# The last of four batches in a one-core adaLN transformer block: second buffers, own PSUM banks, and each engine's order written out call by call

## The chip, the cores and the metric

One core of a Trainium2 chip runs the whole block as one launch. Time is device microseconds from the start to the end of one execution; less is better. The kernel before has a median of 464.82 us over three runs (464.00 to 464.89).

## What is computed

Four batches of 1024 tokens and 512 channels go through attention and a feed-forward step, both behind a layer norm that is scaled and shifted by a modulation vector of the batch, and both added back through a gate:

```python
mod = (silu(c) @ wmod).reshape(4, 6, 1, -1)          # sa, ca, ga, sb, cb, gb
ga, gb = [sign(g) * max(abs(g), 0.25) for g in (ga, gb)]
h = layernorm(x) * (1 + ca) + sa
qf, kf = h @ Wq.T, h @ Wk.T                          # 64 columns each
attn = softmax(16-times-the-same qf @ kf.T)          # one matrix for all 16 heads
x = x + ga * ((attn @ (h @ Wv.T)) @ Wo.T)
h = layernorm(x) * (1 + cb) + sb
x = x + gb * (h @ sum_r(factors[r]) / sqrt(8) + bias)
```

`head_f` is all ones, so every head has the same probabilities, and the kernel works with one probability matrix per batch and one product matrix of Wv and Wo.

## The kernel before

**Tiles.** The 4096 tokens are 32 tiles of 128 rows, eight per batch. Tiles 24 to 31 are the last batch. Every product is made in three matmuls of a `fp32r` upper part and a rest (`three`, L459 to L466: upper by rest, rest by upper, upper by upper), so each operand is kept twice, as `_hi` (rounded, written by ScalarE) and `_lo` (whole minus rounded, written by VectorE, helper line L1062).

**One tile's way.** For tile t: scores (4 matmuls of 512 columns into `ps_s`, two banks, L540 and L541), row maximum on VectorE (`row_max`, L1121), exponentials on ScalarE (`exponentials`, L804, into the single buffer `probs`), then a turn of the probabilities by 90 degrees. It goes through DRAM: one store from SyncE (`send_p`, L401), four loads (`fetch_p`, L409) into one half of `pb`, and a block transpose on VectorE (`turn_p`, L1196). Only tile 24 (and the first few) is turned on TensorE instead. ScalarE rounds the turned probabilities in two halves into `pt_hi` (`probs_part`), VectorE makes `pt_lo` (`probs_rest`), and `attend` runs 24 matmuls with the batch's values into `ps_o`. VectorE scales and gates the sum (`gate_attention`, L1156, into `attn`), adds it to the row in `x_ring` (`add_x`, L1164) and takes the layer norm's statistics (L1169, L1173). GpSimd makes the inverse deviation in three small instructions (`of_x1`, L1470 to L1474), ScalarE normalizes (`normalize_x1`, L830), another store and load through DRAM (L372, L377) and a block transpose (`turn_x1`, L1191) turn the tile, ScalarE modulates it (L756) into `h2_f` and rounds it (`h2_upper`), VectorE makes the rest (`h2_rest`), and `feed_forward` runs 12 matmuls into `ps_y`. ScalarE copies the sum out into the one buffer `ffn` (`ffn_out`, L865), and GpSimd adds the bias, multiplies by the gate and adds the row (`result`, L1487, L1493, L1497). SyncE stores tiles in pairs (`store_pair`, L313).

**What is single.** `ps_s`, `probs`, `ps_o`, `ps_y`, `attn`, `ffn`, `pt_hi`/`pt_lo`, `h2_hi`/`h2_lo` exist once; `v_hi` and `v_lo` hold 16 tiles, those of two batches, so the half of batch 2 is read by nobody once tile 23 has been attended.

**What sets the order.** Each engine runs its own written list and waits on semaphores that count what the others have done. The list is a step per tile. TensorE's step t in the last batch is:

```python
if turned_by_pe(t): transpose_probs(t)        # tile 24 alone
if t > T - TB: scores_of(scored_in(t))        # t + 2; none in step 30
feed_forward(t - 3)
if t == T - TB: scores_of(scored_in(t))
attend(t, g)
```

The other engines' steps of the last batch are `closing_step` on ScalarE and VectorE, `step` on SyncE and GpSimd. Behind step 31 stand the feed-forwards of tiles 29, 30 and 31, the last in two halves of 256 columns in `ps_y` and `ps_o` with VectorE making both parts in four pieces. `gated` (L1181) takes the scaling and the gate of tiles 29, 30 and 31 on VectorE, with the bias times the gate added ahead by GpSimd (`add_gated_bias`, L1515). Tiles 0 to 23 have other work besides: the values and keys of the next batch.

## Time and profile before

| | us |
|---|---|
| median of three runs | 464.82 |
| the profiled execution, its own time | 464.78 |
| its span in the trace | 463.0 |
| TensorE busy in the span | 450.1 |
| VectorE busy | 365.9 |
| ScalarE busy | 338.8 |
| GpSimd busy | 237.7 |

The granted TensorE clock is 1.00 throughout (the higher of its two levels, 2.4 GHz). The profiled execution lasted 1.8 us longer than its span. A matmul row's duration overlaps that of the next one: rows of 0.39 us start 0.23 us apart. So what a stretch of matmuls costs is read from the starts, and a stall is a start that comes later than that.

### The profile page before, as it was taken

Reading aid. Unit: us, or ns where it says so; the run is one execution under the profiler, and the core shown is the slowest. Engines: PE = TensorE matmul, PEld = TensorE weight load, DVE = VectorE, ACT = ScalarE, POOL = GpSimd, SP = SyncE. Lnnn points to the kernel's source line nnn. Section 1 sums busy time; section 2 is a strip of 40 time slices with the busy share of each in tenths; the row PEclk is TensorE's granted clock in tenths of the full one; section 3 lists DMA queues with packets and bytes.
Section 4 is the critical chain, followed back from the end, with each engine's and each line's share of the span. In section 5 each row is a group of like instructions: output and inputs, shape, how many; then the busy total and the mean of one; then the engine's idle time right before and its main releaser. Section 6 shows DMA issues by size and latency. Waiting matters only on the chain. (4 is left out here: it accounts for less than half of the span.)

```text
span 463.0 us, 7344 instructions
## 1 busy us (share of the span) xinstructions
PE 450.1 (97%) x2114; PEld 365.1 (79%) x2114; DVE 365.9 (79%) x641; ACT 338.8 (73%) x676; POOL 237.7 (51%) x307
## 2 busy tenths in 40 slices
PE   8989999999999999999999999999999999999996
PEld 5768778788888888888888888888888777777674
DVE  5988879678777878789787987798887577887765
ACT  5889777687868777778787786878786566567552
POOL 0347546152555554455565645454644475566662
PEclk9999999999999999999999999999999999999999
DMA  7999999634678365867677366877674237565512
GB/s 288 382 356 218 158 177 170 141 74 132 183 206 271 92 206 159 264 203 241 195 195 228 110 216 190 258 201 245 185 227 115 91 117 227 158 217 180 183 58 91
DMA packets 79160, 88.07 MB, mean 190 GB/s; under 512 B 4872, under 2 KB 55816, under 8 KB 79120
## 3 DMA queue, kind: packets, MB, share of 16 engines
q1 hardware_dynamic: 75168, 80.00, 56.5%
q0 software_dynamic: 3808, 7.34, 9.6%
q8 instruction: 17, 0.28, 0.2%
q10 hardware_dynamic: 144, 0.26, 0.2%
q14 instruction: 23, 0.19, 0.1%
HBM read 53.49 MB, written 34.10 MB: 189 GB/s over the span
## 5 line engine op out<-in xcount | busy, mean ns | idle before, releaser
L1470 POOL TENSOR_SCALAR ve<-mv 128x1 f32<-128x1 f32 x64 | 22.5, 351 | 165.7 <-DVE mv L1173 120.1
L464 PE MATMUL ps_o<-v_lo,pt_hi 128*128 128x512 f32 x256 | 100.2, 391 | 0.9 <-DVE pt_lo L1062 0.9
L466 PE MATMUL ps_o<-v_hi,pt_hi 128*128 128x512 f32 x256 | 99.7, 389 | 0.0
L465 PE MATMUL ps_o<-v_hi,pt_lo 128*128 128x512 f32 x256 | 99.6, 389 | 0.0
L1062 DVE TENSOR_TENSOR h_lo<-h_f,h_hi 128x512 fp32r<-128x512 f32 (+1 forms) x67 | 49.7, 741 | 12.2 <-ACT h_hi L728 11.6
L464 PEld LDWEIGHTS ps_o<-v_lo,pt_hi 128*128 128x128 f32 x256 | 48.0, 188 | 12.9 <-issue 2.9
L466 PEld LDWEIGHTS ps_o<-v_hi,pt_hi 128*128 128x128 f32 x256 | 48.0, 188 | 10.1
L465 PEld LDWEIGHTS ps_o<-v_hi,pt_lo 128*128 128x128 f32 x256 | 48.1, 188 | 9.7
L756 ACT ACTIVATE h_f<-x1b,mod_t 128x128 f32<-128x128 f32 x120 | 53.1, 596 | 2.8 <-DVE x1b L1191 2.5
L464 PE MATMUL ps_y<-f_lo,h_hi 128*128 128x512 f32 (+1 forms) x124 | 48.7, 393 | 2.3 <-issue 1.5
L465 PE MATMUL ps_y<-f_hi,h_lo 128*128 128x512 f32 (+1 forms) x124 | 47.9, 386 | 0.0
L466 PE MATMUL ps_y<-f_hi,h_hi 128*128 128x512 f32 (+1 forms) x124 | 47.9, 386 | 0.0
L1472 POOL TENSOR_TENSOR rstd<-ve,minus_half 128x1 f32<-128x1 f32 x64 | 44.8, 700 | 5.3
L756 ACT ACTIVATE h_f<-xb,mod_t 128x128 f32<-128x128 f32 x80 | 35.4, 593 | 12.9 <-DVE xb L1187 12.8
L464 PE MATMUL ps_v<-wvo_lo,h_hi 128*128 128x512 f32 x112 | 44.3, 396 | 0.0
L465 PE MATMUL ps_v<-wvo_hi,h_lo 128*128 128x512 f32 x112 | 43.8, 391 | 0.0
L1196 DVE STREAM_TRANSPOSE pb<-pb 128x1024 f32<-128x1024 f32 x24 | 29.8, 1241 | 17.6 <-DMA pb<-p_blocks 17.6
L466 PE MATMUL ps_v<-wvo_hi,h_hi 128*128 128x512 f32 x112 | 43.6, 390 | 0.0
L1487 POOL TENSOR_TENSOR ffn<-ffn,bias_bc 128x512 f32<-128x512 f32 x29 | 40.2, 1388 | 5.8 <-ACT ffn L865 5.8
L1497 POOL TENSOR_TENSOR x_ring<-ffn,x_ring 128x512 f32<-128x512 f32 x30 | 38.8, 1293 | 5.2 <-POOL ffn L1493 5.0
L1493 POOL TENSOR_TENSOR ffn<-ffn,gates 128x512 f32<-128x512 f32 x29 | 38.8, 1338 | 4.9 <-issue 4.5
L1121 DVE TENSOR_REDUCE negmax<-ps_s 128x1 f32<-128x1024 f32 x32 | 38.8, 1212 | 2.0 <-PE ps_s L541 1.8
(201 smaller groups left out, 1032.2 us busy)
## 6 DMA issues: line engine op xcount, KB each, us to landing
x_blocks<-xn SPq DMA_DIRECT2D x50, 256.0 KB, 2.7
p_blocks<-probs SPq DMA_DIRECT2D x24, 512.0 KB, 3.6
pb<-p_blocks SPq DMA_DIRECT2D x96, 128.0 KB, 3.2
x_ring<-in_x SPq DMA_DIRECT2D x16, 512.0 KB, 4.6
x1b<-x_blocks SPq DMA_DIRECT2D x30, 256.0 KB, 2.9
result<-x_ring SPq DMA_DIRECT2D x15, 512.0 KB, 3.0
f_sum<-in_factors POOLq DMA_DIRECT2D x14, 512.0 KB, 6.2
xb<-x_blocks SPq DMA_DIRECT2D x20, 256.0 KB, 2.9
```

The lines of the kernel that those rows point to most:

```text
L464: nc.tensor.matmul(acc, a_hi, b_lo, start=first, stop=False)
L465: nc.tensor.matmul(acc, a_lo, b_hi, start=False, stop=False)
L466: return nc.tensor.matmul(acc, a_hi, b_hi, start=False, stop=last)
L756: last = nc.scalar.activation(to[:, k, :].rearrange("p (c b) -> p b c", b=Q), turned[:, k], ACT.Identity, scale=mod_t[:, b, v + 1, k:k + 1 ...
L1062: return nc.vector.tensor_tensor(to, whole, full(hi), ALU.subtract)
L1121: nc.vector.tensor_reduce(negmax[:, t & 3:(t & 3) + 1], ps_s[:], AX_X, ALU.max, negate=True).then_inc(max_done, 1)
L1196: nc.vector.transpose(pb[:, n & 1, :], pb[:, n & 1, :]).then_inc(pb_turned, 1)
L1470: nc.gpsimd.tensor_scalar(ve[:, one], mv[:, u, 1:2], EPS, None, ALU.add).then_inc(ve_done, 1)
L1472: nc.gpsimd.tensor_tensor(rstd[:, one], ve[:, one], minus_half[:], ALU.pow).then_inc(rstd_done, 1)
L1487: nc.gpsimd.tensor_tensor(ffn[:], ffn[:], bias_bc[:], ALU.add).then_inc(biased_done, 1)
L1493: nc.gpsimd.tensor_tensor(ffn[:], ffn[:], gates[:, 1, b & 1, :], ALU.mult).then_inc(gated_done, 1)
L1497: nc.gpsimd.tensor_tensor(tile, ffn[:], tile, ALU.add).then_inc(y_done, 1)
```

## The change

Tiles 0 to 23 keep their order on all engines, but for the end of step 23, which is now part of the written-out list. For the last batch:

- `pt_hi`/`pt_lo` of odd tiles get a second home in `v_hi`/`v_lo`, slots 0 and 1; h2's parts rotate over three homes (slots 2 and 3, and the old one); `ffn` alternates with slot 0 of `x_ring`; `rden` has four columns.
- Attention of even tiles goes to `ps_qk`, of odd tiles to `ps_o`; feed-forward of odd tiles from 21 on to `ps_v`, of even ones to `ps_y`, of tile 30 to `ps_t[1]`, and the halves of tile 31 to the two banks of `ps_s`.
- Every engine's calls from the end of step 23 to the end of the kernel are written out one by one.

```diff
+        pt_homes = [(pt_hi[:], pt_lo[:]),
+                    tuple(v[:, 0:2, :].rearrange("p s (j i) -> p (s j) i", i=P) for v in (v_hi, v_lo))]
+        h2_homes = [tuple(v[:, i, :].rearrange("p (k i) -> p k i", i=P) for v in (v_hi, v_lo)) for i in (2, 3)]
+        h2_homes.append((h2_hi[:], h2_lo[:]))
+        ffn_homes = [ffn[:], x_ring[:, 0, :]]
-        last_banks = [ps_y, ps_o]
+        last_banks = [ps_s[:, 0:D // 2], ps_s[:, D:D + D // 2]]
...
+        late = TILES - PER_BATCH
+        def h2_of(t):
+            if t == T - 2:
+                return h2_next_to_last
+            return h2_homes[(t - late + 2) % 3 if t >= late - 2 else 2]
+        def ffn_of(t):
+            return ffn_homes[t % 2 if t >= late - 3 else 0]
+        def y_bank(t):
+            if t == T - 2:
+                return ps_t[1]
+            return ps_v if t >= late - 3 and t % 2 else ps_y
+        def o_bank(t):
+            return ps_qk if t >= late and t % 2 == 0 else ps_o
...
-                wait(pe, attn_done, t)
+                wait(pe, attn_done, t if t < late else t - 1)
...
-                    if j == 3 * TB // 4 and aside is not None:
+                    if j == HALF and aside is not None:
...
+            scores_of(25)
+            transpose_probs(24)
+            feed_forward(21)
+            scores_of(26)
+            attend(24, 12)
+            scores_of(27)
+            feed_forward(22)
+            attend(25, 12)
+            scores_of(28)
+            attend(26, 13)
+            scores_of(29)
+            feed_forward(23)
+            attend(27, 13)
+            scores_of(30)
+            feed_forward(24)
+            attend(28, 14, lambda: scores_of(31))
+            attend(29, 14)
+            feed_forward(25)
+            attend(30, 15, lambda: feed_forward(26))
+            attend(31, 15)
+            feed_forward(27)
+            transpose_last_but_one()
+            feed_forward(28)
+            feed_forward(29)
+            last_transpose()
+            feed_forward(30)
+            last_half(0)
+            last_half(1)
...
-                wait(act, y_acc, t)
+                wait(act, y_acc, t if t < late - 2 else t - 2)
...
-                wait(act, y_done, t)
-                nc.scalar.activation(ffn[:], ps_y[:], ACT.Identity, scale=FSCALE).then_inc(ffn_done, 1)
+                wait(act, y_done, t if t < late - 3 else t - 1)
+                if t == late - 3:
+                    act.wait_ge(y_stored, 16 * (PAIRS // 2 + 1))
+                nc.scalar.activation(ffn_of(t), y_bank(t)[:], ACT.Identity, scale=FSCALE).then_inc(ffn_done, 1)
...
+            def gate_third_last():
+                dve.wait_ge(y_acc, T - 2)
+                dve.wait_ge(y_done, T - 4)
+                gated(ffn_of(T - 3), y_bank(T - 3)[:]).then_inc(ffn_done, 1)
```

SyncE, from the exponentials of tile 25 on. `p_blocks<-probs` is a `send_p`, `pb<-p_blocks` a `fetch_p`, `x_blocks<-xn` a `send_x1`, `x1b<-x_blocks` a `fetch_x1`. Before:

```order
L401 DMA p_blocks<-probs 128x4x256
L409 DMA pb<-p_blocks 32x4x256 x4
L372 DMA x_blocks<-xn 128x4x128
L377 DMA x1b<-x_blocks 128x512
L401 DMA p_blocks<-probs 128x4x256
L409 DMA pb<-p_blocks 32x4x256 x4
L372 DMA x_blocks<-xn 128x4x128
```

Now:

```order
L429 DMA p_blocks<-probs 128x4x256
L437 DMA pb<-p_blocks 32x4x256 x4
L429 DMA p_blocks<-probs 128x4x256
L400 DMA x_blocks<-xn 128x4x128
L405 DMA x1b<-x_blocks 128x512
L437 DMA pb<-p_blocks 32x4x256 x4
L429 DMA p_blocks<-probs 128x4x256
L400 DMA x_blocks<-xn 128x4x128
L437 DMA pb<-p_blocks 32x4x256 x4
L405 DMA x1b<-x_blocks 128x512
```

The probabilities of tile 26 are now sent ahead of the trip of tile 23's rows, and those of tile 27 are fetched ahead of the rows of tile 24.

VectorE, from the gate of tile 23 on. Before:

```order
L1156 SCALAR_TENSOR_TENSOR attn<-ps_o,rden,gates 128x512
L1116 CAST qs_lo<-qk_lo 64x256
L1117 CAST qs_lo<-qk_lo 64x256
L1121 TENSOR_REDUCE negmax<-ps_s 128x1
L1164 TENSOR_TENSOR x_ring<-attn,x_ring 128x512
L1169 BN_STATS stats<-x_ring 128x6
L1173 BN_AGGR mv<-stats 128x2
L1062 TENSOR_TENSOR pt_lo<-ps_t,pt_hi 128x512 x2
L1191 STREAM_TRANSPOSE x1b<-x1b 128x512
L1149 RECIPROCAL rden<-rowsum 128x1
L1121 TENSOR_REDUCE negmax<-ps_s 128x1
L1196 STREAM_TRANSPOSE pb<-pb 128x1024
```

Now:

```order
L1307 SCALAR_TENSOR_TENSOR attn<-ps_o,rden,gates 128x512
L1268 TENSOR_REDUCE negmax<-ps_s 128x1
L1263 CAST qs_lo<-qk_lo 64x256
L1264 CAST qs_lo<-qk_lo 64x256
L1342 STREAM_TRANSPOSE x1b<-x1b 128x512
L1315 TENSOR_TENSOR x_ring<-attn,x_ring 128x512
L1209 TENSOR_TENSOR pt_lo<-ps_t,pt_hi 128x512
L1300 RECIPROCAL rden<-rowsum 128x1
L1320 BN_STATS stats<-x_ring 128x6
L1324 BN_AGGR mv<-stats 128x2
L1268 TENSOR_REDUCE negmax<-ps_s 128x1
L1209 TENSOR_TENSOR pt_lo<-ps_t,pt_hi 128x512
```

The row maximum of tile 25 comes first, and the two halves of `pt_lo` of tile 24 stand apart, one ahead of the statistics and one behind the maximum of tile 26.

VectorE, the last rows of the program. Before:

```order
L1181 SCALAR_TENSOR_TENSOR probs<-ps_v,gates 128x512
L1454 TENSOR_TENSOR x_ring<-probs,x_ring 128x512
L1181 SCALAR_TENSOR_TENSOR attn<-ps_y,gates 128x256
L1460 TENSOR_TENSOR x_ring<-attn,x1b 128x256
```

Now:

```order
L1332 SCALAR_TENSOR_TENSOR probs<-ps_t,gates 128x512
L1414 TENSOR_TENSOR x_ring<-probs,x_ring 128x512
L1332 SCALAR_TENSOR_TENSOR x_ring<-ps_v,gates 128x512
L1332 SCALAR_TENSOR_TENSOR attn<-ps_s,gates 128x256
L1425 TENSOR_TENSOR x_ring<-attn,x1b 128x256
```

The gate of tile 29 (`x_ring<-ps_v`, `gate_third_last`) stood ahead of the four pieces of tile 31 before, and now stands behind tile 30's and ahead of tile 31's halves.

## Rows read from the trace of the kernel before

**Rows 1.** The page, its first line.

```profile
span 463.0 us, 7344 instructions
```

**Rows 2.** Busy time by stretch: window, length, each engine's us (instructions), clock, DMA share, GB/s.

```profile
200.00:360.00 160.00, 159.96 (x748) 133.60 (x747) 134.49 (x228) 125.86 (x253) 85.11 (x113) 1.00 0.68 199
369.60:459.70 90.10, 84.62 (x370) 65.52 (x368) 67.75 (x110) 53.46 (x102) 54.56 (x58) 1.00 0.48 152
```

**Rows 3.** Timeline of TensorE, 358 to 369 us: start, us, what.

```profile
358.74 0.39 PE L464 MATMUL ps_y<-f_lo,h_hi 128*128 128x512 f32 x1
...
361.46 0.39 PE L540 MATMUL ps_s<-k_both,qs_lo 128*128 128x512 f32 x1
...
362.36 0.39 PE L464 MATMUL ps_o<-v_lo,pt_hi 128*128 128x512 f32 x1
...
367.80 0.39 PE L540 MATMUL ps_s<-k_both,qs_lo 128*128 128x512 f32 x1
...
368.71 1.03 PE L470 MATMUL ps_t<-ident,probs 128*128 128x128 f32 x8
```

**Rows 4.** Timeline of TensorE, 370 to 460 us: starts behind a stall, and the last.

```profile
370.58 0.47 PE L464 MATMUL ps_y<-f_lo,h_hi 128*128 128x512 f32 x1 [0.83 <-ACT ffn L865]
...
380.93 0.47 PE L540 MATMUL ps_s<-k_both,qs_lo 128*128 128x512 f32 x1 [0.90 <-ACT probs L804]
...
448.66 0.40 PE L466 MATMUL ps_o<-v_hi,pt_hi 128*128 128x512 f32 x1
...
454.61 0.66 PE L470 MATMUL ps_t<-ident,xn 128*128 128x128 f32 x4 [0.48 <-ACT xn L839]
...
459.44 0.28 PE L465 MATMUL ps_o<-f_hi,h_lo 128*128 128x256 f32 x1
459.56 0.28 PE L466 MATMUL ps_o<-f_hi,h_hi 128*128 128x256 f32 x1
```

**Rows 5.** Timeline of ScalarE, 371 to 376 us.

```profile
371.21 1.12 ACT L804 ACTIVATE probs<-ps_s,negmax 128x1024 f32<-128x1024 f32 x1 [0.78 <-DVE negmax L1121]
...
375.18 0.60 ACT L865 ACTIVATE ffn<-ps_y 128x512 f32<-128x512 f32 x1 [1.78 <-POOL x_ring L1497]
```

**Rows 6.** SyncE's and VectorE's timelines: the trip of tile 25's probabilities.

```profile
372.44 0.36 SPq L401 DMA_DIRECT2D p_blocks<-probs  x1
375.38 1.76 SPq L409 DMA_DIRECT2D pb<-p_blocks  x4
...
379.66 1.25 DVE L1196 STREAM_TRANSPOSE pb<-pb 128x1024 f32<-128x1024 f32 x1 [3.08 <-DMA pb<-p_blocks]
```

**Rows 7.** VectorE's groups, 369 to 460 us: xcount, busy us, mean ns.

```profile
L1062 DVE TENSOR_TENSOR h_lo<-h_f,h_hi 128x512 fp32r<-128x512 f32 x9 | 10.3, 1140 | 3.4 <-ACT h_hi L728 3.4
L1062 DVE TENSOR_TENSOR pt_lo<-pb,pt_hi 128x512 fp32r<-128x512 f32 x14 | 8.8, 671 | 0.0
L1121 DVE TENSOR_REDUCE negmax<-ps_s 128x1 f32<-128x1024 f32 x7 | 8.5, 1210 | 0.1
```

**Rows 8.** Timelines of GpSimd and VectorE at 371 us.

```profile
370.61 1.29 POOL L1487 TENSOR_TENSOR ffn<-ffn,bias_bc 128x512 f32<-128x512 f32 x1 [5.76 <-ACT ffn L865]
...
371.10 1.36 DVE L1164 TENSOR_TENSOR x_ring<-attn,x_ring 128x512 f32<-128x512 f32 x1
```

**Rows 9.** Timeline of all engines, 453 to 463 us.

```profile
453.67 1.27 POOL L1497 TENSOR_TENSOR x_ring<-ffn,x_ring 128x512 f32<-128x512 f32 x1
455.11 0.38 SPq L313 DMA_DIRECT2D result<-x_ring  x1
...
458.44 0.69 DVE L1454 TENSOR_TENSOR x_ring<-probs,x_ring 128x512 f32<-128x512 f32 x1
...
459.95 1.18 SPq L453 DMA_DIRECT2D result<-x_ring  x2
460.34 0.42 DVE L1460 TENSOR_TENSOR x_ring<-attn,x1b 128x256 f32<-128x256 f32 x1
```

**Rows 10.** DMA issues, 440 to 463 us: KB each, median us to landing.

```profile
result<-x_ring SPq DMA_DIRECT2D x1, 512.0 KB, 2.8
```

More of the change, by code:

```diff
@@ L561, in attend @@
                     v = [part[:, first + j, :] for part in (v_hi, v_lo)]
-                    last = three(ps_o[:], (pt_hi[:, j, :], pt_lo[:, j, :]), v, j == 0, j == TB - 1)
+                    last = three(o_bank(t)[:], [part[:, j, :] for part in pt_of(t)], v, j == 0, j == TB - 1)
                 last.then_inc(o_acc, 1)
@@ L583, in feed_forward, with last_half @@
                                  (f_hi[:, k, :], f_lo[:, k, :]), k == 0, k == C - 1)
+                last.then_inc(y_acc, 1)
+            def last_half(half):
+                pe.wait_ge(exp_done, T)
+                for k in range(C):
+                    if half == 0:
+                        pe.wait_ge(last_lo_done, k + 1)
+                    last = three(last_banks[half], [part[:, k, :] for part in h2_of(T - 1)],
+                                 [part[:, k, column_halves[half]] for part in (f_hi, f_lo)], k == 0, k == C - 1)
                 last.then_inc(y_acc, 1)
@@ L621, in step @@
                     ready()
[L622 to L623 removed]
+                attend(t, g)
+                if scored_last_in(t) is not None and t < T - TB - 1:
                     scores_of(scored_last_in(t))
@@ new lines, in _ @@
+            probs_part(26, 0)
+            probs_part(26, 1)
+            modulate_x1(23, batch_of(11))
+            h2_upper(23)
+            exponentials(28)
+            probs_part(27, 0)
+            ffn_out(22)
+            probs_part(27, 1)
+            normalize_x1(25, 1, False)
+            pair_q(15)
+            exponentials(29)
+            modulate_x1(24, batch_of(12))
+            h2_upper(24)
+            probs_part(28, 0)
+            probs_part(28, 1)
+            normalize_x1(26, 0, False)
@@ L1446, in _ @@
[L1446 to L1461 removed]
+            gate_attention(23, 1, 2)
@@ new lines, in _ @@
+            turn_x1(28)
+            gate_attention(30, 0, 3)
+            add_x(30)
+            x1_stats(30, 0)
+            h2_rest(28)
+            invert_sum(31, 1)
+            gate_attention(31, 1, 3)
+            turn_x1(29)
+            add_x(31)
+            x1_stats(31, 1)
+            add_last_bias()
+            h2_rest(29)
+            h2_rest(30, whole=h_f)
+            last_h2_parts(0)
+            last_h2_parts(1)
+            last_h2_parts(2)
+            last_h2_parts(3)
+            gate_next_to_last()
```

451 lines of the change are left out of this document (303 added, 148 removed).

## The prediction

> **What bounds the kernel now.** I first read busy time by stretch [rows 2]. Between 200 and 360 us TensorE is busy 159.96 of 160.00 us. There nothing but fewer matmuls could help, and the change removes none. From 369.6 us, where the last batch's turn on TensorE ends, to 459.7 us, its last matmul, it is busy 84.62 of 90.10 us, while VectorE has 67.75, ScalarE 53.46 and GpSimd 54.56. Busy time hides part of the stalls, since a row's duration overlaps its successor's. The start times in TensorE's timeline tell the true cost [rows 3]: a feed-forward takes 361.46 - 358.74 = 2.72 us, a score product 368.71 - 367.80 = 0.91, an attention 367.80 - 362.36 = 5.44. The eight transposes of tile 24's probabilities end 0.88 us after 368.71.
>
> The matmuls behind 369.6 us are ten feed-forwards (27.2 us), eight attentions (43.5), six score products (5.5), four plus four transposes (0.9) and the two halves of tile 31, 24 matmuls of 256 columns at 459.56 - 459.44 = 0.12 (2.9, [rows 4]): **80.0 us of work in 90.1 us**. The other **10.1 us are stalls**, spread over the batch. Their causes stand in brackets [rows 4]: ScalarE's copy of `ffn`, the exponentials of the tile before, and at 454.61 the normalized last tile, for which little other work was left. The `ffn` chain shows at 375.18 on ScalarE: the copy had waited 1.78 us for GpSimd to give the only `ffn` free [rows 5], and it stands ahead of other ScalarE work. Outside this stretch lie 369.6 us in front and 463.0 - 459.7 = 3.3 us behind: last gate, last sum and the store [rows 1, 4, 9].
>
> **Tiles 0 to 23: no change.** Same calls in the same order under a full TensorE. `rden` grows by 8 bytes per partition; no row gives that a price, and I take 0.
>
> **The matmul stretch.** The change removes and adds no matmul. Its least length is 80.0 us, so the most it can take from this stretch is 10.1. How much of it comes is decided by whether each operand is there when TensorE arrives. I place the calls at a full TensorE and ask the other engines.
>
> - *Feed-forward 21* goes to `ps_v` and waits for the copy of tile 20 only, not that of the tile just ahead. It can start at 369.6; before, it started at 370.58 [rows 4]. Score 26 starts at 372.3. It needs exponential 25, which began at 371.21 [rows 5]; VectorE's maximum now stands ahead of two query copies (0.6 us) and of nothing else, so it ends at about 371.6. On time.
> - *Attention 24* starts at 373.2 instead of 374.34 and needs its second half at 375.9. VectorE does the maximum of tile 26 (1.21 us, [rows 7]) between the halves, from 373.8 when score 26 is in, then the half: ready about 375.6. On time by 0.3.
> - *Attention 25* is due at 382.3. The trip of its probabilities took from 372.44 (store issued) to 379.66 (VectorE starts the turn), 7.2 us [rows 6]. From 371.7 that is 378.9, but VectorE first finishes the gate of tile 24 at 379.65. Turn 1.2, rounding 0.6, rest 0.6, and the add of tile 24's row between: 381.5 to 382.7. Up to 0.4 late.
> - *Attention 26*, due at 389: store behind exponential 26 (376.9), SyncE frees for the loads at 381.5 because the rows of tile 23 are ahead, turned at 387, ready 388.3. *Attention 27*, due at 397.9: ready at 397.0, second half due at 400.6, ready at 400.3. Between 373 and 400 us VectorE has hardly an idle moment.
> - *Attentions 28 to 31* stand 3 us and more behind their probabilities, because the score products run three tiles ahead of the attention by then. The feed-forwards run four to five tiles behind the attention at the dense part, so their inputs are long there, and three homes for h2's parts and two for `ffn` keep ScalarE from waiting for TensorE and GpSimd.
> - *The end*: behind attention 31 there now are feed-forwards 27, 28 and 29, 8.2 us. Before, the way from the last attention matmul at 448.66 to the transposes of tile 31 at 454.61 took 6.0 us [rows 4], with one and a half feed-forwards, 4.1 us, over it. Now 8.2 us cover the 6.0. Tile 31's four modulated pieces, their parts and a gate took from 454.61 to VectorE's sum at 458.44 [rows 4, 9], 3.8 us with the gate (0.69) in it; feed-forward 30's 2.7 lie over it, and only the first of the four pieces is needed by its end.
>
> So the remaining stalls are between 0 and about 3.5 us: four near misses, each late by at most one GpSimd instruction (1.3 us less 0.4 of reserve). I take **1.0 us**, nearer the lower end, because only tile 25 is late in my placing.
>
> **Behind the last matmul.** Before, 3.3 us. Now VectorE has, behind feed-forward 30 (end at 446.7 in a full stretch), the gate and sum of tile 30, the gate of tile 29, and the two halves: three of 0.69 us [rows 9] with their waits, 447.0 to 449.2, then four of 0.42: 450.9, which is 1.3 us behind the last matmul (449.6), against 460.34 + 0.42 - 459.7 = 1.1 before [rows 9]. The new thing is SyncE. GpSimd's add of tile 29 (1.27, [rows 9]) can only start behind that gate, 449.3, ends at 450.6, and the 512 KB store of the pair, which started at 455.11 and so was over at 458 before, is now issued at 450.8, ahead of both last halves in SyncE's order. It lands 2.8 us after issue [rows 10]: 453.6 alone. The halves go out at 451.2 and 451.7, and before, the last of them was issued at 459.95 + 1.18 - 0.35 = 460.8 and the span ended 2.2 us later [rows 1, 9]: 453.9, plus 0.3 for sharing with the pair. Lower bound: the pair is free, 453.7. Upper: the stores queue one behind the other, 455.5. I take 454.2, thus 4.6 behind the last matmul: **+1.3 us**.
>
> **Sum.** The profiled execution took 464.78 us, the median of the runs is 464.82, so they stand together. 464.78 - 10.1 + 1.0 + 1.3 = **457.0 us**.
>
> **VectorE against GpSimd.** One row bears on the size of the remaining stalls: at 371.10 VectorE's sum of two SBUF tiles took 1.36 us, while GpSimd ran from 370.61 to 371.90 [rows 8]; and the batch's nine `h_lo` subtractions, also of two SBUF tiles, mean 1.14 [rows 7], against 0.69 for the sum at 458.44, where GpSimd is idle [rows 9]. The Trainium skill, page "SBUF — State Buffer", section "Who interferes with whom", says that a VectorE instruction with two SBUF inputs and a GpSimd instruction that reads SBUF lock each other out for a whole instruction. The trace agrees: the sum ends 0.56 us behind the GpSimd row's end. By that rule the change could come out worse, since it puts more two-input work of VectorE (half `pt_lo` from `pb`) next to GpSimd work.
>
> **The rivals.**
>
> *Forecast: TensorE all but full.* 457.0, with 455.4 (no stall, tail +0.7) to 458.6 around it. For it: the placing above, and VectorE's 67.75 us fit in 80. Chance 0.60.
>
> *VectorE is held by GpSimd in the dense part.* The fourteen `pt_lo` halves have meant 0.67 us so far, unhindered [rows 7]. If half of them meet a GpSimd instruction and lose 0.5 us each, as the `h_lo` do, 3.5 us more reach TensorE at the places with 0.3 us of reserve: 460.5. Against it: in my placing GpSimd waits for statistics over most of 381 to 400. Chance 0.20.
>
> *The trip through DRAM is late.* SyncE's waits are in order, and tile 26's loads stand behind a load of rows that waits for its own store. If each of the attentions 25 to 27 is 1.2 us later than placed, 457.0 + 3.0 = 460. For it: the four load issues take 1.76 us and the turn waited 3.08 for them [rows 6]. Chance 0.12.
>
> *Slower: a loop over two tiles.* ScalarE's exponential of tile t + 2 stands behind the rounding of tile t's probabilities, which waits for t's trip, which waits for t's exponential. Around it: exponential 1.3, trip 7.2, turn 1.2, rounding 0.6 to 3.0 with a modulation between: 10.3 to 12.7 us for two tiles. TensorE needs 20.0 for two. It would decide from 20 on, and at 23 (1.5 per tile more than TensorE, eight tiles) the stretch is 92 us instead of 90.1: 464.8 + 1.9 + 1.3 = 468. The rows stand far from it. Chance 0.04.
>
> *The stalls only move.* Each of the written-out waits returns what its neighbour gives, and the stretch stays at 89 to 90 us: 464.5. Chance 0.04.
>
> **The numbers.** The likeliest case gives 457.0. From 455.3 to 460.8 lie the forecast and most of the two next cases; what is left out is their upper parts and the last two. A measurement can tell about 0.2%, 0.9 us, from no change: faster 0.93, same 0.03, slower 0.04.
>
> **What the next profile shows.** Right: feed-forward 21 starts 0.9 us ahead of 370.58, attention 24 at 373.2; the last matmul between 449.6 and 451; no stall before the transposes of tile 31; the pair's store issued behind GpSimd's last add and landing with the halves. Wrong if a stall of over 1 us stands ahead of an attention (look whether `pt_lo` or the load is its releaser), if `pt_lo` means over 0.9 us, or if tiles 0 to 23 end at another time than 368.7.

## The result, and the profile after

The changed kernel takes 462.42 us at the median of 20 runs (461.10 to 467.21), the kernel before on the same chip 465.34 (20 runs, 463.58 to 469.71). The ratio is **0.9944, with a 95% interval of 0.9926 to 0.9963: faster by 0.56%**, about 2.9 us. The sign is as forecast; the time lies 1.6 us above the top of the range, and the gain is 2.9 us where the sum promised 7.8.

The page of the kernel after, its span and its busy times:

```profile
span 462.4 us, 7363 instructions
## 1 busy us (share of the span) xinstructions
PE 446.7 (97%) x2114; PEld 364.8 (79%) x2114; DVE 373.6 (81%) x641; ACT 337.7 (73%) x676; POOL 239.4 (52%) x307
```

This profiled execution took 464.23 us, 1.8 above its median, and the reason is not in the last batch. Tiles 0 to 23, whose order is unchanged, had two stalls there that the profile of before did not have. TensorE's timeline, kernel after:

```profile
154.27 0.39 PE L524 MATMUL ps_qk<-h_lo,wqk_hi 128*128 128x256 f32 x1 [1.68 <-DVE h_lo L1209]
```

The start at 154.27 is 1.83 us late, and one at 256.01 is 0.61 late.

Tile 24's transposes end at 372.2 us instead of 369.6; over all profiles of this study that moment lies between 368.9 and 373.1, though no experiment touches the calls ahead of it. So whole spans of single profiles aren't compared below. What is compared is two lengths that start behind it: the **stretch**, from the end of tile 24's transposes to the end of the last matmul (80.0 us of work, as placed in the prediction), and the **tail**, from there to the end of the span. Before, they are 90.1 and 3.3; after, 84.6 and 5.6.

Busy time by stretch, kernel after (columns as in [rows 2]):

```profile
372.20:456.80 84.60, 81.89 (x370) 66.33 (x368) 71.93 (x109) 51.71 (x102) 54.48 (x57) 1.00 0.51 156
```

Against [rows 2], the same 370 matmuls lie in 84.60 us instead of 90.10. VectorE has one instruction fewer and yet is busy 71.93 us instead of 67.75. That is the first sign of what went wrong: its instructions got longer.

TensorE's starts behind a stall, kernel after, which answer to [rows 4]. A start's distance from where the row ahead leaves it free is the stall: 0.73, 0.35, 0.30, 1.03 and 1.08 us.

```profile
372.08 0.48 PE L524 MATMUL ps_v<-f_lo,h_hi 128*128 128x512 f32 x1
...
392.11 0.47 PE L524 MATMUL ps_qk<-v_lo,pt_hi 128*128 128x512 f32 x1 [0.57 <-DVE pt_lo L1209]
...
417.22 0.47 PE L524 MATMUL ps_o<-v_lo,v_hi 128*128 128x512 f32 x1 [0.20 <-DVE v_lo L1209]
...
431.26 0.50 PE L524 MATMUL ps_qk<-v_lo,pt_hi 128*128 128x512 f32 x1
...
448.24 0.60 PE L530 MATMUL ps_t<-ident,xn 128*128 128x128 f32 x4
...
451.42 0.35 PE L524 MATMUL ps_s<-f_lo,v_hi 128*128 128x256 f32 x1
...
452.88 0.38 PE L524 MATMUL ps_s<-f_lo,v_hi 128*128 128x256 f32 x1 [0.87 <-DVE v_lo L1209]
...
454.42 0.39 PE L524 MATMUL ps_s<-f_lo,v_hi 128*128 128x256 f32 x1 [0.92 <-DVE v_lo L1209]
...
456.65 0.28 PE L526 MATMUL ps_s<-f_hi,v_hi 128*128 128x256 f32 x1
```

Feed-forward 21 starts without a stall, and so do the transposes of tile 31 at 448.24 and every score product: the three stalls that [rows 4] showed are gone. Three short stalls are in the middle, ahead of attention 26, attention 29 and the second half of attention 30. Two long ones stand between the last halves' matmuls, where the forecast had none, and both wait for a `v_lo` of VectorE. From 451.42 to the end at 456.77 the 24 matmuls take 5.35 us, instead of 2.9. The first of the four casts at that place in the kernel before, then VectorE's and GpSimd's timelines there, kernel after:

```profile
455.79 0.23 DVE L1135 CAST h_hi<-h_f 128x128 fp32r<-128x128 f32 x1 [2.22 <-ACT h_f L1051]
```

```profile
449.36 0.59 DVE L1293 CAST v_hi<-h_f 128x128 fp32r<-128x128 f32 x1 [1.89 <-ACT h_f L953]
449.99 1.29 DVE L1209 TENSOR_TENSOR v_lo<-h_f,v_hi 128x128 fp32r<-128x128 f32 x1
451.20 1.30 DVE L1293 CAST v_hi<-h_f 128x128 fp32r<-128x128 f32 x1
...
452.74 1.30 DVE L1293 CAST v_hi<-h_f 128x128 fp32r<-128x128 f32 x1
...
457.26 1.31 DVE L1425 TENSOR_TENSOR x_ring<-attn,x1b 128x256 f32<-128x256 f32 x1
```

```profile
449.83 1.30 POOL L1739 TENSOR_TENSOR x_ring<-x_ring 128x512 f32<-128x512 f32 x1
451.08 1.33 POOL L1730 TENSOR_TENSOR ffn<-ffn,gates 128x512 f32<-128x512 f32 x1
452.59 1.36 POOL L1739 TENSOR_TENSOR x_ring<-ffn,x_ring 128x512 f32<-128x512 f32 x1 [0.18 <-POOL ffn L1730]
457.03 1.26 POOL L1739 TENSOR_TENSOR x_ring<-x_ring 128x512 f32<-128x512 f32 x1 [3.07 <-DVE x_ring L1332]
```

The rows of 1.29 to 1.31 on VectorE are instructions that take 0.22 to 0.43 elsewhere, and each ends 0.1 to 0.3 us behind a GpSimd instruction: 451.28 beside 451.13, 452.50 beside 452.41, 454.04 beside 453.95, 458.57 beside 458.29. GpSimd is at work on tiles 27 and 28 there, back to back, because the new order puts their feed-forwards behind attention 31. The chain of work that ended last, in the profile after, runs through the casts at 451.20 and 452.74 and the sum at 457.26.

SyncE's timeline at the end, kernel after ([rows 9] before), the pair's store and the two halves; then the DMA issues from 440 us on ([rows 10] before), KB each and median us from issue to landing:

```profile
458.45 0.37 SPq L341 DMA_DIRECT2D result<-x_ring  x1
458.88 1.33 SPq L513 DMA_DIRECT2D result<-x_ring  x2
```

```profile
result<-x_ring SPq DMA_DIRECT2D x2, 512.0 KB, 2.8
...
result<-x_ring SPq DMA_DIRECT2D x2, 128.0 KB, 2.6
```

The store of tiles 28 and 29 (L341) goes out first, as placed, and both halves (L513) go out behind it.

### The profile page after: what moved, and what is told of

Same layout as the page of the kernel before. It is cut to its first block, busy times and chain, and to the rows that moved or that the text cites. A ratio compares the mean times of both kernels' runs of the same rounds, so it can differ in the third digit from the quotient of the medians.

```text
span 462.4 us, 7363 instructions
## 1 busy us (share of the span) xinstructions
PE 446.7 (97%) x2114; PEld 364.8 (79%) x2114; DVE 373.6 (81%) x641; ACT 337.7 (73%) x676; POOL 239.4 (52%) x307
## 4 chain that ended last, share of the span: by engine, by line
PE 64%; DMA 17%; DVE 7%; ACT 5%; issue 3%; SPq 3%; POOL 1%; DVEq 0%; POOLq 0%; ACTq 0%
PE ps_o L526 7%; PE ps_o L524 7%; PE ps_o L525 7%; DMA x_blocks<-xn 6%; PE ps_v L524 5%; PE ps_v L525 5%; PE ps_v L526 5%; DMA xb<-x_blocks 4%; PE ps_y L524 3%; PE ps_y L526 3%; PE ps_y L525 3%; PE ps_qk L524 2%; PE ps_s L600 2%; PE ps_s L601 2%; PE ps_qk L526 2%
## 5 line engine op out<-in xcount | busy, mean ns | idle before, releaser
L524 PE MATMUL ps_o<-v_lo,pt_hi 128*128 128x512 f32 x192 | 74.7, 389 | 0.0
L526 PE MATMUL ps_o<-v_hi,pt_hi 128*128 128x512 f32 x192 | 74.7, 389 | 0.0
L525 PE MATMUL ps_o<-v_hi,pt_lo 128*128 128x512 f32 x192 | 74.7, 389 | 0.0
L1209 DVE TENSOR_TENSOR h_lo<-h_f,h_hi 128x512 fp32r<-128x512 f32 x57 | 41.7, 732 | 10.1 <-ACT h_hi L821 9.6
L524 PEld LDWEIGHTS ps_o<-v_lo,pt_hi 128*128 128x128 f32 x192 | 36.0, 188 | 7.6
L525 PEld LDWEIGHTS ps_o<-v_hi,pt_lo 128*128 128x128 f32 x192 | 36.0, 188 | 7.5
L897 ACT ACTIVATE probs<-ps_s,negmax 128x1024 f32<-128x1024 f32 x32 | 35.4, 1107 | 8.9 <-DVE negmax L1268 8.6
L821 ACT ACTIVATE v_hi<-ps_v 128x512 fp32r<-128x512 f32 x28 | 16.8, 598 | 29.1 <-PE ps_v L526 28.9
L1711 POOL TENSOR_SCALAR nmr<-mv,rstd 128x1 f32<-128x1 f32 x64 | 27.6, 432 | 14.1 <-POOL rstd L1709 13.9
L524 PE MATMUL ps_y<-f_lo,h_hi 128*128 128x512 f32 x88 | 34.4, 391 | 0.1
```

Source lines behind the costliest of these rows:

```text
L524: nc.tensor.matmul(acc, a_hi, b_lo, start=first, stop=False)
L525: nc.tensor.matmul(acc, a_lo, b_hi, start=False, stop=False)
L526: return nc.tensor.matmul(acc, a_hi, b_hi, start=False, stop=last)
L897: nc.scalar.activation(to, source, ACT.Exp, bias=negmax[:, t & 3:(t & 3) + 1], accum_out=rowsum[:, t & 3:(t & 3) + 1]).then_inc(exp_done, 1)
L1209: return nc.vector.tensor_tensor(to, whole, full(hi), ALU.subtract)
L1711: nc.gpsimd.tensor_scalar(nmr[:, one], mv[:, u, 0:1], rstd[:, one], -1.0, ALU.mult, ALU.mult).then_inc(nmr_done, 1)
```

## The experiments

One theory stood behind the first three: *the pieces of tile 31 are held by GpSimd's work on tiles 27 and 28*. Its rivals were that VectorE is held in the dense part, and that the mid-batch stalls come from the trip through DRAM or from VectorE's own order. A second theory was that the tail is long because VectorE's gate of tile 29, the pair's store and the halves now stand on each other. The undo runs ask what the second homes and banks are worth. The whole account follows. Stretch and tail are from one profile each. The ratios are against the kernel before on the same chip; its median was 465.34 beside the kernel after, 464.63 beside the next four rows, 465.60 beside the four undo rows and 466.09 beside the last four. So the ratios, not the medians, compare one group with another:

| kernel | stretch | tail | sum | median | ratio, interval |
|---|---|---|---|---|---|
| before | 90.1 | 3.3 | 93.4 | 465.34 | 1 |
| after | 84.6 | 5.6 | 90.2 | 462.42 | 0.9944 (0.9926 to 0.9963) |
| no bias and gate on GpSimd, tiles 27, 28 | 82.5 | 5.1 | 87.6 | 459.63 | 0.9899 (0.9866 to 0.9932) |
| the same for tiles 24 to 28 | 82.8 | 5.1 | 87.9 | 460.48 | 0.9903 (0.9866 to 0.9939) |
| tile 31's pieces by way of PSUM | 82.6 | 6.2 | 88.8 | 460.88 | 0.9924 (0.9887 to 0.9960) |
| gate of tile 29 early | 87.8 | 3.4 | 91.2 | 462.38 | 0.9945 (0.9920 to 0.9971) |
| one attention bank | 89.5 | 5.6 | 95.1 | 467.43 | 1.0015 (0.9971 to 1.0059) |
| one feed-forward bank | 89.7 | 5.6 | 95.3 | 465.77 | 0.9988 (0.9950 to 1.0026) |
| one home for `pt` | 91.0 | 5.6 | 96.6 | 468.99 | 1.0054 (1.0018 to 1.0090) |
| all three undone | 103.8 | 5.6 | 109.4 | 480.62 | 1.0273 (1.0178 to 1.0369) |
| pieces by PSUM and gate 29 early | 82.3 | 5.4 | 87.7 | 459.38 | 0.9865 (0.9817 to 0.9913) |
| with gate 28 on VectorE too | 83.6 | 3.4 | 87.0 | 459.79 | 0.9846 (0.9801 to 0.9892) |
| with two orders changed too | 81.8 | 3.4 | 85.2 | 458.14 | 0.9826 (0.9774 to 0.9878) |
| the two orders alone | 85.4 | 4.3 | 89.7 | 461.70 | 0.9897 (0.9860 to 0.9934) |

Two cautions on reading it. One stall varies by itself: that ahead of attention 26 is between 0.44 and 1.67 us in seven kernels with the same calls up to there (the kernel after, the four rows behind it, and the two of the last four that keep the order). It follows the moment at which VectorE can start the turn of tile 26, 16.9 to 18.1 us behind tile 24's transposes. So differences of the stretch under 1 us need the rows to explain them. And the intervals of the four rows behind the kernel after overlap with its own: what these four show of the cause, they show in their rows, not in their times.

### GpSimd's bias and gate left out, tiles 27 and 28

```diff
+        bare = (27, 28)
...
             def add_bias(t):
+                if t in bare:
+                    return
...
             def gate_result(t, b):
+                if t in bare:
+                    return
```

> Leaves out GpSimd's bias and gate of tiles 27 and 28 (four instructions of 1.3 us), so these two tiles lack bias and gate. Theory A, GpSimd's backlog behind attention 31 holds VectorE's casts and subtractions of the last tile: the casts fall from 0.85 to 0.22 us, the four pieces take about 2 us instead of 5.4 (449.4 to 454.8), TensorE has no stall of about 1 us between the pieces, and the median is 2.5 to 4 us below the changed kernel's 462.4, at 458.4 to 460. Rival B, ScalarE's modulation and the order of the pieces set the pace: pieces still 4 us or more, median 462 to 463. Rival C, the lower clock in the last microseconds is the cause: the granted clock in the last slice and the time stay as they are.

VectorE's timeline, this kernel, the place of the pieces:

```profile
449.75 0.23 DVE L1294 CAST v_hi<-h_f 128x128 fp32r<-128x128 f32 x1 [1.89 <-ACT h_f L954]
...
451.15 0.22 DVE L1294 CAST v_hi<-h_f 128x128 fp32r<-128x128 f32 x1
451.40 0.29 DVE L1210 TENSOR_TENSOR v_lo<-h_f,v_hi 128x128 fp32r<-128x128 f32 x1
```

The eight instructions take 449.75 to 451.69, 1.9 us instead of 5.4, the two stalls at the end are gone, and the stretch is 2.1 us shorter. With no GpSimd beside it (its busy time from 449.7 to 451.7 is 0.00), a cast costs 0.22 instead of 1.30. VectorE's busy time in the stretch falls from 71.93 to 68.46. The tail stays long, as the sum of the first half still meets GpSimd's add of tile 29.

### The same, tiles 24 to 28

The edit is `bare = (24, 25, 26, 27, 28)`.

> Leaves out bias and gate of tiles 24 to 28 on GpSimd. Theory A holds for the middle of the batch too: VectorE's holds at 404.6 (cast 1.28), 405.9 (1.67) and 415.5 (two of 1.6) shrink, stalls of 0.35 and 0.30 us ahead of attentions 29 and 30 go, 0.5 to 1 us less than the kernel without 27 and 28. Rival (the trip of the probabilities through DRAM sets the stalls in the middle): the same time as that kernel, and the 0.7 us stall ahead of attention 26 stays under both, since no GpSimd sum of these tiles runs there.

The stretch is 82.8, no better than the run before. The stalls ahead of attention 26 and of attention 30's second half stay, at 0.44 and 1.32 us, so GpSimd's bias and gate of these tiles don't make them. One group of VectorE, 369 to 452 us, this kernel (count, busy us, mean ns):

```profile
L1210 DVE TENSOR_TENSOR v_lo<-pb,v_hi 128x512 fp32r<-128x512 f32 x8 | 7.4, 930 | 0.1
```

The mean of 930 ns is that of the kernel after (931), and it isn't spread over the group. Six of the eight rows take 0.66 to 0.69, and two stand in one record of VectorE's timeline, here beside GpSimd's gate and add of tile 23, which this edit leaves in:

```profile
412.00 3.28 DVE L1210 TENSOR_TENSOR v_lo<-pb,v_hi 128x512 fp32r<-128x512 f32 x2
```

```profile
411.75 1.29 POOL L1735 TENSOR_TENSOR x_ring<-x_ring,gates 128x512 f32<-128x512 f32 x1
413.22 1.51 POOL L1746 TENSOR_TENSOR x_ring<-x_ring 128x512 f32<-128x512 f32 x1 [0.18 <-POOL x_ring L1735]
```

Both halves of tile 29's parts, 1.3 us by [rows 7], took 3.28, and attention 29 is late by 0.35 in this kernel as in the kernel after. So of the three stalls in the middle this one belongs to GpSimd's hold by the overlap of the rows. No run moved that GpSimd work, so it is read, not tried.

### Tile 31's pieces by way of PSUM

ScalarE writes the modulated piece into a free PSUM bank and rounds it from there; VectorE is left with the subtraction, which now has one input in PSUM.

```diff
+        piece_banks = [ps_o, ps_qk, ps_y, ps_o]
...
-                nc.scalar.activation(h2_f[:, k, :], ps_t[0][:, P * k:P * (k + 1)], ACT.Identity,
+                nc.scalar.activation(piece_banks[k][:, 0:P], ps_t[0][:, P * k:P * (k + 1)], ACT.Identity,
...
+            def last_upper(k):
+                act.wait_ge(h2_f_done, T + k)
+                act.wait_ge(y_acc, T - 4)
+                rounded(h2_of(T - 1)[0][:, k, :], piece_banks[k][:, 0:P]).then_inc(last_hi_done, 1)
...
-                nc.vector.tensor_copy(hi, h2_f[:, here, :]).then_inc(last_hi_done, 1)
                 dve.wait_ge(last_hi_done, k + 1)
-                rest(lo, h2_f[:, here, :], hi).then_inc(last_lo_done, 1)
+                rest(lo, piece_banks[k][:, 0:P], hi).then_inc(last_lo_done, 1)
```

> Complete computation. The last tile's modulated pieces go to free PSUM banks, ScalarE makes the upper part instead of a VectorE cast, VectorE's subtraction then has one SBUF input only. Theory A: VectorE's four subtractions take 0.3 us each though GpSimd works beside them, the last piece is ready about 2 to 2.5 us behind the first modulation instead of 5.4, no stall between pieces; 2 to 3 us less than 462.4: 459.4 to 460.4. Rival B: ScalarE, with eight instructions of 0.4 us in a row instead of four, is the pace: 3.2 us for the pieces and a gain of 1 us or less.

VectorE's and GpSimd's timelines, this kernel:

```profile
448.88 0.29 DVE L1217 TENSOR_TENSOR v_lo<-ps_o,v_hi 128x128 fp32r<-128x128 f32 x1 [2.23 <-ACT v_hi L822]
449.50 0.29 DVE L1217 TENSOR_TENSOR v_lo<-ps_qk,v_hi 128x128 fp32r<-128x128 f32 x1 [0.33 <-ACT v_hi L822]
...
451.76 1.79 DVE L1419 TENSOR_TENSOR x_ring<-probs,x_ring 128x512 f32<-128x512 f32 x1
```

```profile
449.00 1.29 POOL L1744 TENSOR_TENSOR x_ring<-x_ring 128x512 f32<-128x512 f32 x1
...
451.72 1.29 POOL L1744 TENSOR_TENSOR x_ring<-ffn,x_ring 128x512 f32<-128x512 f32 x1 [0.18 <-POOL ffn L1735]
```

This is the cleanest test of the mechanism, since GpSimd does all its work here. A subtraction that reads one operand from PSUM takes 0.29 at 449.50 in the middle of a GpSimd instruction; the one that reads two SBUF tiles took 1.29 in the kernel after. The Trainium skill, page "SBUF — State Buffer", section "Who interferes with whom", says that an instruction of VectorE with at most one SBUF input, outside the modes that use both ports, doesn't contend with GpSimd, and that copies and casts can enter such a mode. Both halves of that agree with the rows: 0.29 for the PSUM form, and 0.22 or 1.30 for the cast. The edit also takes the casts off VectorE, so the rows show the subtraction freed, and the casts are freed by being elsewhere. The pieces now come 0.63 us apart, which is ScalarE's pace (0.42 and 0.28, overlapping a little), and TensorE doesn't wait. The stretch gives back 2.0, and the tail takes 0.6 of it: VectorE's sum of tile 30 took 1.79 us instead of 0.69, since GpSimd's add of tile 28 had begun 0.04 us before it.

### The gate of tile 29 ahead of the pieces

```diff
+        third_last = probs[:, D:2 * D]
...
-                dve.wait_ge(y_done, T - 4)
-                gated(ffn_of(T - 3), y_bank(T - 3)[:]).then_inc(ffn_done, 1)
+                dve.wait_ge(p_out, 16 * trips_of(T))
+                gated(third_last, y_bank(T - 3)[:]).then_inc(third_gated, 1)
...
+            gate_third_last()
             last_h2_parts(0)
...
             add_next_to_last()
-            gate_third_last()
             gate_half(0)
```

> Complete computation. VectorE gates tile 29 ahead of the last tile's pieces, into the free half of the probabilities' buffer, so the store of tiles 28 and 29 no longer stands ahead of the last halves. The tail behind the last matmul was 5.6 us, before it was 3.3. Theory: the late gate is 1.5 to 2 us of it (0.6 on VectorE, 1 in SyncE's order and the shared transfer); the pair's store is issued near 455.3 instead of 458.4 and the end comes 1 to 1.5 us earlier, 461.0 to 461.4. Rival: the tail is VectorE's held sum (1.31 us instead of 0.42 at 457.3) alone, which also goes away here since GpSimd is done by then, and the pair's store counts for nothing: then the last halves still land 2.6 us after issue.

The tail is 3.4 again, as before the change, and the last halves land in 1.7 us instead of 2.6. But the stretch became 87.8, and the time didn't move (0.9945 beside 0.9944). TensorE's timeline and its windows, this kernel:

```profile
451.28 0.28 PE L528 MATMUL ps_s<-f_hi,v_hi 128*128 128x256 f32 x1
453.44 0.42 PE L526 MATMUL ps_s<-f_lo,v_hi 128*128 128x256 f32 x1 [1.88 <-DVE v_lo L1211]
453.66 0.41 PE L527 MATMUL ps_s<-f_hi,v_lo 128*128 128x256 f32 x1
```

```profile
451.00:453.30 2.30, 0.56 (x3) 0.35 (x3) 2.27 (x2) 0.00 (x0) 2.23 (x2) 1.00 0.28 105
453.40:457.20 3.80, 3.77 (x18) 3.72 (x18) 2.46 (x6) 0.00 (x0) 0.00 (x0) 0.55 0.60 223
```

GpSimd's add of tile 29 now follows that of tile 28 at once, so one more piece is held: two VectorE instructions of 1.30 and 1.25 us stand between 450.80 and 453.38. TensorE stalls for 2.04 us, and behind that its granted clock is 0.55, near the lower of its two levels (1.2 GHz). The last 18 matmuls stand 0.21 us apart instead of 0.12 and take 1.6 us more. The tail was mended and the bill came in the stretch. That tells why the two repairs belong together, which later runs try.

### Undoing the second homes and banks, one at a time

Attention in one bank:

```diff
         def o_bank(t):
-            return ps_qk if t >= late and t % 2 == 0 else ps_o
+            return ps_o
...
-                wait(pe, attn_done, t if t < late else t - 1)
+                wait(pe, attn_done, t)
```

> Undoes one part: all attentions in one PSUM bank, the written order as in the changed kernel. Theory, each second home pays where the dense order puts like behind like: attention 29 must wait for the gate of 28 and attention 31 for that of 30, which VectorE does 1 to 2.5 us after the last matmul; 3 to 4 us longer from tile 24's transposes to the last matmul (84.6 us in the changed kernel). Rival, the order alone brings the gain: within 0.5 us of 84.6.

The sum is 4.9 us longer. TensorE's timeline at attention 29, and its clock behind it, this kernel:

```profile
417.54 0.39 PE L526 MATMUL ps_o<-v_hi,pt_hi 128*128 128x512 f32 x1
420.41 0.77 PE L524 MATMUL ps_o<-v_lo,v_hi 128*128 128x512 f32 x1 [2.48 <-DVE attn L1307]
...
421.40 0.63 PE L526 MATMUL ps_o<-v_hi 128*128 128x512 f32 x1
421.82 0.63 PE L524 MATMUL ps_o<-v_lo,v_hi 128*128 128x512 f32 x1
```

```profile
420.40:423.40 3.00, 2.99 (x7) 2.44 (x8) 2.60 (x4) 1.36 (x4) 3.00 (x3) 0.50 1.03 314
424.40:427.40 3.00, 3.00 (x15) 2.49 (x14) 1.45 (x3) 1.13 (x3) 1.28 (x3) 1.00 0.75 227
```

With one bank, the next attention waits for VectorE to empty it, and VectorE's `attn` stood behind the same pair of held `v_lo` halves (3.26 us from 416.39). The stall is 2.64 us, and behind it the clock is 0.50 for 3 us: 7 matmuls lie in a window that holds 15 at the higher level. By the starts, stall and slow matmuls cost about 4 us. Attention 31, the other place expected, waits 1.11 us. Attention 26 waits 1.77 in this profile, 1.0 more than in that of the kernel after; no edit shows why.

Feed-forward in one bank (`y_bank` gives `ps_y` for all but tile 30, and `feed_forward` waits for the copy of the tile just ahead):

> Undoes one part: feed-forwards 21 to 29 in one PSUM bank. Theory: feed-forwards 28 and 29 wait for the copies of 27 and 28 out of the bank (ScalarE is late with 27's, behind four other calls), 2 to 3 us longer to the last matmul; those before it hardly wait. Rival, the order alone: within 0.5 us of 84.6.

5.1 us longer, most of it at one place: feed-forward 21 starts at 375.69, 2.56 us behind the transposes, since ScalarE's copy of tile 20 (374.94) stands behind a rounding and an exponential in the new order. The clock is then 0.50 from 377.20 to 379.80. The two places that the expectation named are there too, 1.63 us ahead of feed-forward 28 and 0.94 ahead of 29, but in return the two stalls between the last halves' matmuls are gone.

One home for the probabilities' parts (`pt_of` always gives the first home, and the rounding waits for the attention just ahead):

> Undoes one part: the turned probabilities' parts have one home, so ScalarE rounds tile t's only behind the end of attention t - 1. Theory: attentions 29 and 31 follow 28 and 30 with nothing between, and wait for rounding and subtraction, 2 to 2.5 us each: 4 to 5 us longer to the last matmul. Rival, the order alone: within 0.5 us of 84.6.

6.4 us longer, with five stalls ahead of the end: ahead of attention 26 (1.37, within that stall's own spread), attention 29 (1.76), the second half of attention 30 (1.25), attention 31 (1.76) and the transposes of tile 30 (0.69). Ahead of attention 29, ScalarE's first rounding (416.64) is released by the last matmul of attention 28, and rounding and subtraction then lie open.

All three together, the new order alone:

> Undoes all three: one bank for attention, one for the feed-forward, one home for the probabilities' parts; only the order and h2's and ffn's homes stay. Theory: the waits overlap (attentions 29 and 31 wait for the longer of theirs), 6 to 8 us more than 84.6, so at or above the 90.1 of the kernel before. Rival, the order alone brings the gain: under 86.

The window over its whole stretch, this kernel:

```profile
369.40:473.20 103.80, 87.81 (x370) 70.28 (x368) 69.47 (x109) 52.17 (x102) 50.70 (x57) 0.93 0.41 127
```

19.2 us longer than the kernel after, more than the 16.4 that the three take singly and than the 6 to 8 expected, and 2.7% slower than the kernel before (three executions). The stalls grow to 5.24 us (ahead of attention 31), and the mean clock of the stretch is 0.93. The order is written for the homes: it puts feed-forwards and attentions of neighbouring tiles next to each other, which one bank turns into waits. So the order is no gain without the homes and banks. The other half, the homes and banks under the old order, was not run. Nor are h2's three homes and `ffn`'s two undone here.

### The repairs together

The pieces by way of PSUM and the early gate of tile 29:

> Complete computation: the two edits of pieces through PSUM and early gate of tile 29 together. If the end's loss is the lock between VectorE and GpSimd plus the late store: last matmul 82 to 83 us behind tile 24's transposes (84.6 in the changed kernel), 3.4 to 4.5 us behind it (5.6), together 3 to 4 us less than the changed kernel's 90.2; median 458.5 to 459.5. If the store only waits for something else, the part behind the last matmul stays over 5.

Then also tile 28's gate on VectorE, straight out of PSUM, with its bias times the gate added ahead, so that GpSimd has two instructions less at the end and one more earlier:

```diff
+            def gate_28():
+                dve.wait_ge(y_acc, T - 3)
+                dve.wait_ge(y_done, T - 5)
+                dve.wait_ge(ffn_done, T - 4)
+                gated(ffn_of(T - 4), y_bank(T - 4)[:]).then_inc(ffn_done, 1)
...
+            gate_28()
             h2_rest(30, whole=h_f)
+            gate_third_last()
```

> As the one before, and VectorE gates tile 28 from PSUM where it is idle, with its gated bias added ahead on GpSimd, so GpSimd has two instructions less at the end. Theory: VectorE's sum of tile 30 is no longer held (1.79 us instead of 0.7 with the pieces in PSUM), another 0.5 to 1 us behind the last matmul. Rival: the new GpSimd instruction ahead of tile 29's statistics delays that tile, and feed-forward 29 comes late: 0.5 us or more lost there.

Then also two places of the order. SyncE loads tile 26's probabilities ahead of the rows of tile 23, for whose store it has to wait; VectorE makes the second half of tile 30's parts ahead of tile 31's turn:

```diff
-            fetch_x1(23, 1)
             fetch_p(26)
+            fetch_x1(23, 1)
...
-            turn_p(31)
             x1_stats(29, 1)
             probs_rest(30, 1)
+            turn_p(31)
```

> As the one before, and two calls moved: on VectorE the turn of tile 31's probabilities goes behind the second half of tile 30's parts, on SyncE tile 26's probabilities are fetched ahead of tile 23's rows. Theory: the stalls ahead of the second half of attention 30 (0.3 to 1.3 us in the runs so far) and of attention 26 (0.4 to 1.3) go: 81 to 81.7 us to the last matmul, 1 us less than the one before, median 457 to 458.5. Rival: the trip through DRAM takes its time whatever the order, attention 26 stalls as before.

And these two places alone, on the kernel after:

> The changed kernel with only those two calls moved. Theory: the stalls ahead of attention 26 and of attention 30's second half go or shrink to under 0.3 us, 83.6 to 84 us to the last matmul instead of 84.6; the end (two stalls of 1 us, 5.6 us behind the last matmul) stays: median about 1 us below 462.4. Rival: no difference, 84.6.

The first gives 459.38 us. Its tail is still 5.4, since VectorE's sum of tile 30 meets GpSimd's add again. With the gate of tile 28 moved the tail is 3.4, though the times can't tell these two apart (0.9865 and 0.9846). Its stretch is 1.3 us longer, of which 1.0 is the stall of attention 26, far ahead of the edit; the rival, a late feed-forward 29, is not in the rows. The full set gives 458.14, ratio 0.9826 (0.9774 to 0.9878), **the best version found**: 1.2% under the kernel after by the ratios, whose intervals don't touch. Its interval overlaps with those of the two steps ahead of it. VectorE's timeline at its end, the full set:

```profile
451.71 0.69 DVE L1427 TENSOR_TENSOR x_ring<-probs,x_ring 128x512 f32<-128x512 f32 x1
```

The sum that took 1.79 takes 0.69, and the stretch is 81.8 for 80.0 of work. The stalls left are 0.35 ahead of attention 29, 0.52 ahead of a group of transposes at 441.14 and 0.29 at 447.84.

The two orders alone removed the stall of attention 30. That of attention 26 is 0.52 instead of 0.73 us, which is within its own spread: SyncE issued the loads 1.0 us earlier, but VectorE could start the turn only 0.2 us earlier. Yet the stretch was 85.4 instead of the expected 83.6 to 84. TensorE's timeline and windows, this kernel:

```profile
452.51 0.58 PE L524 MATMUL ps_s<-f_lo,v_hi 128*128 128x256 f32 x1 [0.93 <-DVE v_lo L1209]
...
453.10 0.41 PE L526 MATMUL ps_s<-f_hi,v_hi 128*128 128x256 f32 x1
```

```profile
452.50:456.20 3.70, 3.69 (x18) 3.64 (x18) 3.46 (x7) 0.00 (x0) 1.08 (x1) 0.56 0.19 71
```

The same two stalls at the end as in the kernel after, 1.01 and 1.09 us, this time let the clock fall to 0.56, and the last 18 matmuls took 3.7 us instead of the 2.35 that they took in the kernel after (454.42 to 456.77). These 1.35 us are most of what is missing from the expected stretch. They cost the whole nothing, though: VectorE's held sum of the first half ended at 456.67, behind the last matmul (456.20), so the tail shrank by 1.3. The sum of both is 0.5 us less than in the kernel after, as the two shorter stalls say (0.2 and 0.3).

## Why the prediction was right and wrong, point by point

**The bound and the work: right.** 80.0 us of matmuls and stalls above it: the best version's stretch is 81.8. "Tiles 0 to 23: no change" fits the medians, whose 2.9 us are nearly all in the two lengths behind tile 24's transposes (3.2). It doesn't hold for a single profile, since these tiles aren't steady between executions.

**Feed-forward 21, score 26, attentions 24 and 25: right.** Feed-forward 21 starts without a stall, and attention 24 at 375.81, 3.6 us behind the end of tile 24's transposes, as placed (373.2 against 369.6). Undoing the feed-forward's bank put 2.56 us back at just this place. Attention 25, the one that I placed late by up to 0.4, came in time.

**Attention 26: wrong.** I placed it ready 0.7 ahead of its due time; it was 0.73 late. VectorE's timeline, kernel after:

```profile
389.33 1.25 DVE L1347 STREAM_TRANSPOSE pb<-pb 128x1024 f32<-128x1024 f32 x1 [1.39 <-DMA pb<-p_blocks]
390.50 0.67 DVE L1342 STREAM_TRANSPOSE x1b<-x1b 128x512 f32<-128x512 f32 x1
...
391.27 0.69 DVE L1209 TENSOR_TENSOR pt_lo<-pb,pt_hi 128x512 fp32r<-128x512 f32 x1
```

The turn began where I had put it (387, plus the 2.6 by which all of this profile is later, is 389.6). What I left out is VectorE's order behind it: the turn of tile 23's rows and a reciprocal stand ahead of the subtraction, 0.8 us by their starts. The trip through DRAM is the other part. VectorE had waited 1.39 us for the loads, and in other profiles the turn begins up to 1.0 us later still. The full set, with the loads moved ahead, has no stall here, but the two orders alone, with the same move, have 0.52: no run shows that the move is what took it away.

**"Attentions 28 to 31 stand 3 us and more behind their probabilities": wrong for 29 and 30**, by 0.35 and 0.30 us. The first is the pair of held halves, as read from the overlap of the rows. The second is the turn of tile 31 ahead of tile 30's second half; the two orders alone took it away.

**Tile 31's pieces: the step that failed.** The prediction put it as "Tile 31's four modulated pieces, their parts and a gate took from 454.61 to VectorE's sum at 458.44 [rows 4, 9], 3.8 us with the gate (0.69) in it; feed-forward 30's 2.7 lie over it". Its durations were those of a profile in which GpSimd's last instruction began at 453.67 [rows 9] and the pieces came behind it. The change moves three feed-forwards to the end, and with them the results of tiles 27 and 28 onto GpSimd beside the pieces. The casts and subtractions took 449.36 to 454.8, and the stretch paid: 5.35 us for the halves instead of 2.9. Taking GpSimd's work away there and taking VectorE out of its way both removed the stalls and 2.0 to 2.1 us of the stretch. So this part of the expected gain, about half of what is missing, was spent there; the rest is in the sizes below.

**The sizes.** Of the term "−10.1 + 1.0" the trace has 5.5 us less, so 4.6 us remain of stalls and slow restarts instead of 1.0. In them are 2.5 at the end (shown by the two edits), 1.4 in the three stalls of the middle, and 0.7 in starts that come 0.1 us late behind a stall or a transpose. The tail is 2.3 longer instead of 1.3. Together −3.2 us in the profiles, and −2.9 in the medians, against −7.8: 3.6 us missing in the stretch and 1.0 in the tail.

**The tail: right in kind, short by 1.0.** The pair's store did go out ahead of both halves, and they landed together. What I had priced was the queue; what I hadn't is that GpSimd's add of tile 29 (457.03) holds VectorE's sum of the first half for 1.31 us instead of 0.43, and so everything behind it. With the gate early the tail is 3.4; that edit takes away the hold and the late store at once, so their shares are read from the rows and not tried apart.

**The rivals.** *VectorE held by GpSimd in the dense part* had the right mechanism with the wrong place and the wrong instructions. I looked for it in the `pt_lo` halves, of which one pair was held (0.35 us for TensorE); it stood in the casts and subtractions of the last tile and in the sums behind the last matmul. My test for it, a mean of `pt_lo` above 0.9 us, was met by the eight halves in the second home (931 ns) and not by all fourteen (0.82 us, with six of 670 ns), and what lifted it was a single record of two. A mean tells little. Of my other signs of being wrong only the end of tiles 0 to 23 came up, and none of them looked at the pieces of tile 31. I had also taken the rule for instructions with two SBUF inputs alone, while casts with a single one were held as long (1.30 us beside 1.29). *The trip late* had some part in the one stall ahead of attention 26, 0.73 us in this profile and up to 1.67 in others with the same calls up to there. I had priced it at 1.2 for each of three attentions; 25 and 27 came in time. The loop over two tiles and the stalls that only move did not come.

## What to carry to other kernels

When a change moves one engine's work into a stretch where another was alone, durations read from the old profile no longer hold for the pair: for each VectorE instruction on the path to the end, ask what GpSimd does at that moment in the new order, and let the critical ones read an operand from PSUM, or let ScalarE do them. A second buffer and the order that uses it are one change: the order alone cost time here, 2.7% against the kernel before. And price a long TensorE stall above its length, because what follows it may run at the lower clock.
